# Reordering the GpSimd list in the token loop of an attention and expert kernel

## What is computed

```python
xn = _layernorm(x, axis=-1)
x = x + attn(xn, Wq, Wk, Wv, Wo, bo) + ffn(xn, router_w, expert_w1, expert_w2)

# attn: 16 heads of 16. Heads 0..3: softmax attention in windows of 128 tokens, each window seeing
# itself (causally) and the one before. Heads 4..15: causal linear attention in chunks of 64:
#   q = softmax(q); k = elu(k) + 1
#   ctx = cumsum over chunks of k^T v, divided by cumsum of k, shifted by one chunk; out = q ctx
# then out @ Wo + bo
# ffn: 8 experts, top 2 of the router's scores, softmax of the two as gates
#   out += gelu(xf @ expert_w1[e].T) @ expert_w2[e].T * w_e
```

## Time and profile before

| what | value |
|---|---|
| device time, median of 3 runs | 831.96 us (829.16 to 837.24) |
| profiled execution, its own time | 835.22 us |
| its span, first to last instruction | 833.4 us |
| first stage, of this | 0 to about 428.7 us |
| mean granted PE clock | 0.936 |
| busy: PE, DVE, ACT, POOL | 713.3, 422.1, 407.0, 426.0 us |
| PE busy from 45.69 to 195.76 us | 118.61 of 150.07 us |
| PE busy from 428.65 us to the end | 384.21 of 404.75 us |

### The profile page before, as it was taken

The page is one execution under the profiler, slowest core; times in us unless marked ns, Lnnn a source line. Parts: engine busy times, 40 slices in busy tenths (PEclk is TensorE's granted clock), DMA queues, the critical chain, the costliest instruction groups (busy, mean ns, idle before and its releaser), DMA issues.

```text
span 833.4 us, 21487 instructions
## 1 busy us (share of the span) xinstructions
PE 713.3 (86%) x6866; PEld 560.7 (67%) x6867; DVE 422.1 (51%) x1540; ACT 407.0 (49%) x1115; POOL 426.0 (51%) x423
## 2 busy tenths in 40 slices
PE   1978787878679888887879999999999999999983
PEld 0645454545446555565558888888888888888763
DVE  6756565637776777756433333333333333334321
ACT  4756565656336666664533444444444444443331
POOL 6664646455335555557332555555555555544422
PEclk9988888989767999998869999999999999999998
DMA  7424231222211322222112444444444444443321
GB/s 246 127 80 125 71 109 60 94 71 71 63 53 39 83 81 80 82 85 84 42 48 47 77 76 76 76 76 76 76 76 76 76 76 76 77 70 59 58 45 20
DMA packets 87991, 64.26 MB, mean 77 GB/s; under 512 B 54675, under 2 KB 81556, under 8 KB 87924
## 3 DMA queue, kind: packets, MB, share of 16 engines
q1 hardware_dynamic: 73204, 43.69, 19.2%
q0 software_dynamic: 13632, 18.91, 14.2%
q10 hardware_dynamic: 1088, 0.79, 0.3%
HBM read 36.08 MB, written 17.96 MB: 65 GB/s over the span
## 4 chain that ended last, share of the span: by engine, by line
SPq 37%; issue 24%; POOL 17%; PE 9%; DVE 5%; DMA 5%; ACT 2%; POOLq 0%; DVEq 0%; ACTq 0%
SPq L688 36%; PE bank L279 4%; POOL stage L832 3%; POOL state L837 3%; POOL xb L825 2%; PE bank L1105 2%; POOL w2h L740 2%; DMA out<-attn,rows_to 2%; POOL atl L822 1%; POOL w2l L841 1%; DMA out<-res,rows_to 1%; POOL ke L815 1%; PE bank L1213 1%; POOL w1l L841 1%; DVE stats L1240 1%
## 5 line engine op out<-in xcount | busy, mean ns | idle before, releaser
L279 PE MATMUL bank<-stage,w1h 128*128 128x256 f16 (+1 forms) x1248 | 197.4, 265 | 4.9 <-DMA stage<-xin 3.6
L279 PE MATMUL bank<-stage,w1l 128*128 128x256 f16 (+1 forms) x624 | 163.7, 264 | 0.0
L1213 PE MATMUL bank<-w2h,pt 128*128 x568 | 154.9, 273 | 5.9 <-issue 4.8
L1213 PE MATMUL bank<-w2h,spare 128*128 x568 | 154.8, 273 | 0.0
L1213 PE MATMUL bank<-w2l,pt 128*128 x568 | 154.8, 273 | 0.0
L279 PEld LDWEIGHTS bank<-stage,w1h 128*128 x1248 | 114.4, 98 | 23.9 <-issue 7.5
L1024 ACT ACTIVATE pt<-ss 128x512 f16<-128x512 f32 (+1 forms) x78 | 41.8, 583 | 168.8 <-PE bank L1213 164.2
L874 POOL DMA_INDIRECT out<-res,rows_to x36 | 63.1, 1753 | 74.1 <-DMA stage<-rows 52.6
L874 POOL DMA_INDIRECT out<-attn,rows_to x35 | 61.0, 1744 | 73.0 <-DMA out<-attn,rows_to 46.2
L822 POOL TENSOR_TENSOR atl<-attn,ath 128x128 f16<-128x128 f32 x32 | 13.8, 430 | 165.3 <-ACT ath L957 165.3
L949 ACT ACTIVATE ss<-ss,negmax 128x256 f32<-128x256 f32 x128 | 63.5, 497 | 16.0 <-DVE negmax L1301 15.9
(11 more groups left out here) (242 smaller groups left out, 1679.0 us busy)
## 6 DMA issues: line engine op xcount, KB each, us to landing
stage<-w1c SPq DMA_DIRECT2D x16, 512.0 KB, 3.6
stage<-w2c SPq DMA_DIRECT2D x16, 512.0 KB, 3.5
w1h<-x SPq DMA_DIRECT2D x16, 256.0 KB, 3.8
xn_rows<-w2h SPq DMA_DIRECT2D x32, 128.0 KB, 3.2
xb<-x SPq DMA_DIRECT2D x32, 128.0 KB, 3.3
out<-res SPq DMA_DIRECT2D x32, 128.0 KB, 3.5
stage<-xin SPq DMA_TRANSPOSE x144
stage<-rows SPq DMA_TRANSPOSE x140
```

Source lines behind the costliest of these rows:

```text
L279: ins = pe.matmul(dst, lhs(a, k), rhs(c, k), start=(n == 0), stop=(n == len(terms) - 1))
L1213: ins = pe.matmul(bY[h][:, 0:D], (hh, hl)[a][:, f, h * P:(h + 1) * P], (w2h, w2l)[c][:, DS(which * (FC * D) + f * D, D)], start=(f == a == ...
```

## The change

POOL's list in a step is written in another order: the local rows' low half moves from third place to behind the mask and ahead of the weights' subtraction. The instructions, their operands and their waits are the same.

```diff
                     if t.has(-2):
                         b = t.row(-2)
-                        t.wait(s["loch_in"], -2)
-                        t.wait(s["pr_ps"], -4)
-                        pool.tensor_tensor(atl[b][:, 2 * P:3 * P], attn[b][:, 0:P], ath[b][:, 2 * P:3 * P],
-                                           ALU.subtract).then_inc(s["locl_in"], 1)
                         t.wait_dma(xb_loaded, -2)
                         pool.tensor_tensor(xb[b][:], xb[b][:], bias[:], ALU.add).then_inc(s["xb_in"], 1)
                     for u in t.early(1):
...
                         t.wait(s["lin_ps"], -3)
                         pool.tensor_tensor(state[b][:], raw[b][:], ctx_mask[:].unsqueeze(1).to_broadcast([P, 2, CTX]),
                                            ALU.mult).then_inc(s["mask_in"], 1)
+                    if t.has(-2):
+                        b = t.row(-2)
+                        t.wait(s["loch_in"], -2)
+                        t.wait(s["pr_ps"], -4)
+                        pool.tensor_tensor(atl[b][:, 2 * P:3 * P], attn[b][:, 0:P], ath[b][:, 2 * P:3 * P],
+                                           ALU.subtract).then_inc(s["locl_in"], 1)
                     if t.has(0):
                         t.wait(s["stage_up"], 0)
                         pool.tensor_tensor(lo[:, DS(t.window(0) * F, F)], stage[m][:], hi[:, DS(t.window(0) * F, F)],
```

## The result

The kernel after takes 805.96 us (median of 4 runs, 803.6 to 807.24) beside 834.28 for the kernel before on the same chip (829.16 to 837.24): a ratio of 0.966, with the interval 0.960 to 0.972. Forecast were 806 us and a ratio of 0.969.

What follows compares the result with a forecast made beforehand. The prediction took a loop of PE, ACT and POOL, with PE waiting for POOL's mask, as the bound. Its terms, -41.5 + 1.5 + 23 - 9.5 = -26.5 us, gave 806 us from a median of 831.96; range 786 to 827.

Steps and rivals of the forecast that it cites:

- PE's own need, 9.90: Steps 3 to 13: PE alone, at full clock and without waiting for the mask, needs 9.90 us a step.
- the step of 10.15: Steps 3 to 11: with DVE's normalization held by POOL, a step takes 10.15 us instead of 9.90.
- part 1: Steps 3 to 13, with step 2's idle time: the wait for the mask and the low clock go, minus 41.5 us.
- the lock catches L1253: Steps 3 to 11: the port lock holds DVE's two fp32 normalization instructions behind POOL's scaling and mask; step 10.15 us, otherwise 9.90.
- Part 2: Steps 14 to 17: DVE's router sets these, the earlier mask gains nothing, POOL's instructions change places beside it; plus 1.5 us.
- Part 3: Steps 18 to 26: three one-hot pairs are held behind mask, low half and subtraction, delaying PE; plus 23 us.
- the term on top: Steps 18 to 26: first one-hot batch meeting bias and scaling, plus returning low clock; 0.9 us a step, making 12.8.
- Part 4: Steps 27 to 34: waits for the mask go and step 30's gathers start earlier; minus 9.5 us.
- the lock costs little: Rival: PE's idle time goes everywhere, steps 3 to 13 take 9.9 us; minus 64, 768 us, chance 0.12.
- the low clock stays: Rival: steps 3 to 13 keep the low clock, 10.15 + 1.25 us each; 819 us in all, chance 0.15.
- the mask isn't what holds PE: Rival: `qgt` or `atl` is late for PE's first work of a step; time stays at 832, chance 0.07.
- The slower case: Rival: lock bites twice, 14.7 us a step in steps 18 to 26, 11.9 in 3 to 11; 845 us, chance 0.09.

Runs made afterwards that it cites:

- filler matmuls: Kernel before, with 36 matmuls that nothing reads behind PE's step in steps 2 to 12, filling its wait for the mask: 816.39 us, ratio 0.983.
- only the bias ahead: Kernel before, with the bias alone moved ahead of the low half in POOL's list: 811.8 us, ratio 0.973.
- order by step: Kernel after, with the low half just ahead of the mask up to step 27 and behind it from step 28 on: 772.39 us, ratio 0.928.
- quarter subtraction: Kernel after, with the weights' subtraction cut to 256 of 1024 columns in steps 17 to 27: 786.86 us, ratio 0.946.
- waiting subtraction: Kernel after, with POOL waiting in steps 17 to 27 for the step's one-hots before the weights' subtraction: 781.21 us, ratio 0.939.
- the best order, with one wait more: Order by step, with the weight scaling also waiting for the first three pairs of one-hots in steps 17 to 27: 764.03 us, ratio 0.920.

## Why the prediction was right, point by point

**What bounds steps 3 to 13.** Right. PE's wait for the mask went, and the low clock with it. The filler matmuls show these as two terms, 26.5 and 15.8 us.

**PE's own need, 9.90, and the step of 10.15.** The need was 0.3 too high: a step in which nothing holds DVE takes 9.62 (steps 12 and 13, and nearly all of 3 to 13 with the low half just before the mask). The lock's share on top was right: forecast 0.25, measured 9.84 - 9.62 = 0.22. The size of PE's own need is most of the 3.2 us by which part 1 came out better.

**That the lock catches L1253.** The prediction says that no row has L1253 under a POOL instruction. The trace of the kernel before has one, in step 1:

```profile
31.32 1.53 DVE L1253 TENSOR_SCALAR w1h<-w1h,mv,rstd 128x256 f32<-128x256 f32 x2
...
31.62 1.09 POOL L832 TENSOR_SCALAR stage<-stage 128x1024 f32<-128x1024 f32 x1
```

The longer of the two took 1.13 us and ended 0.15 after L832. So this could have been read and not only derived. After the change the same holds in every step from 2 to 11: the two took 1.80 us or more instead of 0.71, each with its end 0.15 us behind one of POOL's. "SBUF — State Buffer", section "Who interferes with whom", in the Trainium skill has DVE and GpSimd share ports under a lock for the length of an instruction, and leaves out reductions. The trace agrees: `qmax`, a reduction from PSUM, took 0.35 and 0.34 us, and `qsum`, a reduction from SBUF, took 0.34 under L843.

**Part 2, plus 1.5.** Wrong in sign: -3.3. The step that failed is that the earlier mask gains nothing here. Before, PE stood 1.77 us for the mask at the end of step 14. This step takes 10.52 us in both kernels with the old order (before and fillers), 9.67 with only the bias ahead (where PE stands 0.92), and 8.67 to 8.95 in the nine others. So 1.8 of the 3.3 us are the mask's. For steps 15 to 17 nothing is shown: they take 51.47 us before and 50.05 after, but two kernels with the same lists up to step 27 took 50.81 and 52.44 (low half just before the mask, and order by step), one profiled execution each. The router's instructions were held about as long as before, by other instructions of POOL's: without the one-hots, their 49 instructions take 21.1 us before and 21.4 after.

**Part 3, the held one-hots.** The mechanism and its place were right. The old place in these steps alone gives the loss back, a shorter subtraction gives most of it back, and so does a subtraction that waits. From the end of `raw` (309.63 in step 25) to `tok1` (314.51) it took 4.88 us, forecast 5.0. Mis-sized was the term on top, 0.9 for the first batch and the clock. In step 25 `raw` ended 7.59 into the step instead of 6.08, and the next step began 1.37 after `tok1` instead of 0.81: 2.1 us. Over the nine steps the mean is less, 13.29 against 12.8, which is 4.4 us in all.

**Part 4, minus 9.5.** The terms that the prediction lists for it add up to 9.1. Steps 28 and 29 (10.24 and 10.19 to 8.57 and 8.51) came as forecast, 3.3 us beside 3.2. Step 27 gained nothing (10.24 to 10.55), since the low clock that follows the idle time at the end of step 26 lies in it (3.4 us); at a clock of 1.00 throughout it took 9.69 and 9.79 (quarter subtraction, waiting subtraction). Step 30 fell from 16.38 to 13.12, where 0.9 was forecast. Three windows of this step, of the kernel before, of the one with fillers and of the kernel after, show what that is:

```profile
380.93:397.31 16.38, 12.49 (x91) 8.61 (x91) 7.62 (x25) 5.91 (x19) 11.68 (x11) 0.73 0.26 83
363.22:377.24 14.02, 10.13 (x92) 6.78 (x92) 7.61 (x25) 5.29 (x18) 11.69 (x11) 0.88 0.32 96
356.99:370.11 13.12, 10.13 (x92) 6.80 (x91) 7.14 (x27) 6.97 (x25) 10.80 (x11) 0.87 0.34 103
```

The first two have the same lists in this step, and PE stands the same 3.20 us for ke in both; but behind it the clock was low for 10.2 us in the one and for 3.4 in the other. At the same clock the change is worth the forecast 0.9 us (14.02 to 13.12). The other 2.4 are the length of the low clock in the profiled execution of the kernel before, which nothing in the order is shown to set. It reached into step 31 as well: 10.74 before, 10.05 with fillers and 7.82 after, so that some 0.7 of its 2.9 us are the clock's and 2.2 the wait for the mask (2.17 forecast). So some 3 of the 30.2 us between the two profiles aren't shown to be the change's. From step 32 to the second stage it is 18.54 us instead of 20.60, 2.1 less, where 0.8 was forecast for the wait and 1.0 for the clock. The wait before step 33 went, but PE's wait for `lrow` behind it grew from 0.58 to 2.29, so that 1.7 of the 1.9 us stayed, and not 1.1. What shortened step 32 besides (1.7 us) was not taken apart.

**The second stage keeps its length.** Nearly: 2.0 us longer. The profile shows PE's two longest waits for a transfer at 2.35 and 1.94 us instead of 1.90 and 1.35, and behind the second a stretch at the low clock around 767 us. From step 33 on, every shorter kernel takes 416 to 419 us instead of 414.3. One part is PE's wait for `lrow` behind the expert table, which now lies open (1.7 us); the cause of the rest stays open.

**The rivals.** That the lock costs little would have needed steps of 9.1 us in 18 to 26; that the low clock stays, 11.4 in 3 to 13. Neither came. That the mask isn't what holds PE fell with PE's wait for it. The slower case wanted 14.0 a step in 18 to 26, and 13.29 is not far from it; but its other half, 11.9 in steps 3 to 11, never came near: there DVE has two instructions to lose, not six, and `qmax`, fed from PSUM, starts under the low half (110.52 beside 110.40) instead of behind it.

**The signs in the profile.** Both of the normalization's instructions are stretched (0.86 and 1.02 us), where one of two was foretold, and the longest L505 takes 2.17 us and not about 3: the delay of some 3 us is spread over three one-hots.

## What to carry to other kernels

Work that waits belongs behind the work that others wait for, but the engine so freed then runs its next long instruction somewhere else: before moving it, list what the partner on the same memory ports issues in that place. Here the same reorder was worth 42 us where that list was short and cost 27 where it held six small instructions; the best order, with one wait more, took 764 us. A wait for something that isn't needed can be the cheapest tool, if the engine that waits has time to spare. And count a change like this one stretch by stretch from the same instruction: the total of -30 us says nothing of the +27 in it.

## What the runs showed of the hardware

**One turn each.** With both lists full, DVE got exactly one of the instructions that are held between two of POOL's, however short it was. A 128x128 fp16 instruction of 0.25 us took 0.95 beside the mask, 2.17 beside the subtraction. So a series of small DVE instructions beside long POOL ones pays POOL's lengths, one for each, until one of the lists has a gap. In all nine steps of 18 to 26 it was the same three: L505 under the mask, L506 under the low half, L505 under the subtraction. After POOL's end these fp16 ones needed 0.04 us more, and the fp32 ones of the normalization 0.15.

**Not every instruction on SBUF is held.** The prediction's wording, that a DVE instruction which reads and writes SBUF stands, is too wide. `qsum` (0.34 us under L843) and the reciprocals (L1363, 0.18 us under L828) read and write SBUF and ran at their usual length. And POOL's `rstd` (L798, 128x2, 0.72 us) held nothing: a normalization instruction that began and ended within it took 0.41.

**Short stops can cost the clock.** PE's stops of 2.6 us in a step of 13.7 brought 3.4 us at 1.2 GHz in every step of 3 to 13, and stops of 1.94 us in 8 of 11 steps. Stops of 1.15 us before steps 19 to 27 and of 1.60 before steps 28 and 29 brought none. The price was 1.3 to 1.4 us a step, on top of the stop itself. The same stop need not cost the same: 3.20 us in step 30 brought 10.2 us at the low clock in one kernel and 3.4 in another with the same list.
